# Combine weights and running decay sums turned by VectorE's block transposition and stored in 128-byte pieces

## Chip, cores and metric

The kernel runs on one core of a Trainium2 chip. The time is the device time of one execution in microseconds (us), as the median of several runs. The core's engines work side by side, each on its own list of instructions, and wait for each other through semaphores: TensorE (PE in the profile; PEld is its weight load), VectorE (DVE), ScalarE (ACT), GpSimd (POOL) and SyncE (SP), which here issues DMAs.

## What is computed

32 sequences of 512 tokens and 256 channels go through two residual layers. The first is a state-space mixer; two of its steps matter here: the running sums of the decays, and the factors `exp(sum[l] - sum[s])` built from them. The second layer is a mixture of 16 experts with a shared expert; here the combine weights matter, one per token and expert, which scale the hidden rows of each expert.

```python
Adt = (dt * A)...; Acs = jnp.cumsum(Adt, axis=-1)
Lmat = jnp.exp(segsum(Adt))                      # exp(Acs[l] - Acs[s]) for s <= l
Y_diag = jnp.einsum('bcln,bcsn,bhcls,bcshp->bclhp', Cr, Br, Lmat, xdt)
...
topk_idx, w, _scores = _route(xf, router_w, correction_bias)
combine = jnp.zeros((S, E), xf.dtype).at[jnp.arange(S)[:, None], topk_idx].add(w)
h = _silu(g) * u
hw = h * combine.T[:, :, None]
routed = jnp.einsum('esh,ehc->sc', hw, down_w)
```

## The kernel before

Each engine has a list of steps written out by hand, in stages: `lead`, `first`, 30 steady iterations (one ahead of a loop, 29 in it), `tail`, `drain`, `last`. A steady iteration overlaps three things: the projection of the query for sequence i+1 (part p), the mixer of sequence i (part a), and the experts of sequence i-1 (part f). So every step below runs 32 times, 30 of them in steady iterations. Sequences are split into 4 chunks of 128 tokens; there are 8 heads and 16 experts.

The order of the work on each engine is the order in its `iteration()`. PSUM banks are handed out in turn: `PLANS` lists the fillings of each part, and the filling at place n takes bank n modulo the number of banks (three for a, two for f), after the one that had the bank before was read out (`slot`).

Two small tensors have to be turned, because they arrive with tokens on the partitions and are needed as rows that a DMA can spread over all partitions:

- The decay sums. TensorE's `cumulate` (L1518 to L1520) makes three products into one bank: the sums by token, the totals by a matrix of ones, and the sums again as rows (32 rows of 128 tokens, L1520). VectorE's `evac_acs` copies the rows to `acsT` (L1138), and SyncE's `decay_store` writes them with one DMA to `acs_row` in device memory (L486). `decay_rows` loads them back into `seg`, broadcast over the partitions (L492); GpSimd's `mask` (L607) and ScalarE's `exp_seg` (L845) follow, then VectorE's product with `CBs` (L1167) and TensorE's `diagonal` (L1577). VectorE's `chunk_y` copies out its result (L1193 for the first chunk), and GpSimd's `gated` (L622) goes on from there.
- The combine weights. VectorE's `route_experts` ends with the weights in `gt`, 128 tokens by 4 chunks by 16 experts (L1303). TensorE's `combine_by_expert` turns them with four transposes (L1611) into an f bank `cT`; ScalarE's `evac_cT` copies them to `cT`, a part of `cb` (L895); SyncE's `combine_store` writes them to `c_row` (L497), and `combine_rows` loads, for each block of two experts, the rows back into `cb` (L505). GpSimd's `combine(j)` (L647) multiplies the hidden rows of block j by them.

Around these steps stand, for each of the 12 hidden blocks j: TensorE's `gate(j)` and `up(j)` (L1443 into an f bank), ScalarE's SiLU and VectorE's `up(j)` (L1249), ScalarE's rounding `round_hidden(j)` (L914), GpSimd's `rest(j)` (L652), and TensorE's `down(j)` (L1632). GpSimd's list in the iteration runs `rest(3); combine(4); gated(0); combine(5); ...` to `rest(10); rest(11)`, all in order. At the start of the next iteration TensorE makes `ffn_by_channel` (the transposes of L1462 into f banks).

Of the kernel before, what the change touches and what calls it, by code (L numbers as in the profile page):

```python
# [12 lines left out]
P = 128  # L13
# [5 lines left out]
SB = SH // P  # L19
LAST = 2  # L20
# [12 lines left out]
def build(nc, x, wq_t, wzx_t, conv_w, conv_b, dt_bias, a_log, d_param, npw, ngw, wo_t,  # L33
# [6 lines left out]
    with ctx:  # L40
# [52 lines left out]
        acsT = sb("acsT", [NT * HS, P])  # L93
# [14 lines left out]
        cT = cb[0:E, 0, :]  # L108
# [38 lines left out]
        class Plan:  # L147
# [7 lines left out]
            def filled_count(self, part, engine, upto=None):  # L155
# [56 lines left out]
                    ("cT", "ACT", "ACT"), ("U4", "DVE", "DVE"), ("G5", "ACT", "ACT"), ("U5", "DVE", "DVE"),  # L212
# [7 lines left out]
                    "G0", "G1", "G2", "G3", "G4", "cT", "G5", "G6", "G7", "G8", "G9", "G10", "G11"),  # L220
# [24 lines left out]
                    ("U2", "DVE", "DVE"), ("G3", "ACT", "ACT"), ("U3", "DVE", "DVE"), ("cT", "ACT", "ACT"),  # L245
                    ("G4", "ACT", "ACT"), ("U4", "DVE", "DVE"), ("G5", "ACT", "ACT"), ("U5", "DVE", "DVE"),
# [7 lines left out]
                    "G0", "G1", "G2", "G3", "cT", "G4", "G5", "G6", "G7", "G8", "G9", "G10", "G11"),  # L254
# [9 lines left out]
                    ("G3", "ACT", "ACT"), ("U2", "DVE", "DVE"), ("cT", "ACT", "ACT"), ("G4", "ACT", "ACT"),  # L264
# [5 lines left out]
                    "G0", "G1", "G2", "G3", "cT", "G4", "G5", "G6", "G7", "G8", "G9", "G10", "G11"),  # L270
# [10 lines left out]
        class Way:  # L281
# [34 lines left out]
            "seg_free": ("SP", "a", NT, True), "acs_stored": ("SP", "a", 16, False),  # L316
# [25 lines left out]
            "cT_ready": ("SP", "f", 1, False), "c_stored": ("SP", "f", 16, False),  # L342
# [17 lines left out]
            "c_ready": ("PE", "f", 1, False), "acc_free": ("PE", "f", 1, True),  # L360
# [95 lines left out]
        def _(sp):  # L456
# [27 lines left out]
            def decay_store():  # L484
                sp.wait_ge(sem["acsT_ready"], 1)
                sp.dma_start(acs_row, acsT[:]).then_inc(sem["acs_stored"], 16)  # L486

            def decay_rows(c):
                sp.wait_ge(sem["acs_stored"], 16)

                sp.wait_ge(sem["seg_free"], now("seg_free", c - 1) if c >= 2 else NT - 1 + c)
                sp.dma_start(seg[:, c % 2, :, :].rearrange("p b c -> p (b c)"),  # L492
                             rows(acs_row, [[0, P], [1, HS * P]], c * HS * P)).then_inc(sem[f"seg_loaded{c}"], 16)

            def combine_store():
                sp.wait_ge(sem["cT_ready"], 1)
                sp.dma_start(c_row, cT).then_inc(sem["c_stored"], 16)  # L497

            def combine_rows(r):
                if r == 0:  # L500
                    sp.wait_ge(sem["c_stored"], 16)
# [251 lines left out]
        def _(act):  # L753
# [139 lines left out]
            def evac_cT():  # L893
                way.filled(act, "ACT", "cT")
                own.do(A.copy(cT, way.bank("cT")[0:E, :]))  # L895
                act.sem_inc(sem["cT_ready"], 1)
                freed["f"].append("cT")
                act.sem_inc(sem["f_out_ACT"], 1)

# [65 lines left out]
            def iteration(g=True):  # L965
# [7 lines left out]
                gate(4); evac_CB(); silu_z(2, 1); exp_table(); decays(); evac_cT(); exp_seg(0); round_hidden(3)  # L973
# [11 lines left out]
            def tail():  # L985
# [6 lines left out]
                conv_first(3); silu_z(2, 1); evac_cT(); round_hidden(3); gate(4); conv_silu(3); silu_z(3, 1)  # L992
# [9 lines left out]
            def drain():  # L1002
                begin("drain")
                f_high(0); f_high(1); score_tanh(); gate(0); gate(1); final_norm(); round_hidden(0)
                round_hidden(1); gate(2); gate(3); round_hidden(2); evac_cT(); gate(4); round_hidden(3)
# [25 lines left out]
        def _(dve):  # L1031
# [252 lines left out]
            def route_experts():  # L1284

                for t in range(NT):
# [16 lines left out]
                V.tensor_tensor(gt[:].rearrange(te, t=NT), gt[:].rearrange(te, t=NT),  # L1303
                                ws[:].unsqueeze(2).broadcast_to([P, NT, E]), ALU.mult).then_inc(sem["c_ready"], 1)
# [102 lines left out]
        def _(pe):  # L1407
# [105 lines left out]
            def cumulate():  # L1513
# [5 lines left out]
                nc.tensor.matmul(b[:, n:2 * n], ones[:], rhs, start=True, stop=True)  # L1519
                fill("acs", nc.tensor.matmul(b[0:n, P:2 * P], rhs, upper[:], start=True, stop=True))  # L1520
# [157 lines left out]
            def iteration(g=True):  # L1678
# [8 lines left out]
                gate(4); CB(); x_by_token(0); up(3); down(1); x_by_token(1); combine_by_expert(); down(2)  # L1687
                settled("c_ready"); up(4); gate(5); state(0); project_z(3, 1); diagonal(0); up(5)
# [11 lines left out]
            def tail():  # L1700
# [6 lines left out]
                project_z(2, 1); down(1); combine_by_expert(); gate(4); settled("c_ready"); project_z(3, 1)  # L1707
# [10 lines left out]
            def drain():  # L1718
# [3 lines left out]
                down(0); settled("acc_free"); up(2); down(1); combine_by_expert(); gate(4); settled("c_ready")  # L1722
# [71 lines left out]
```

## Time and profile before

| | us |
|---|---|
| median of 3 runs | 3145.26 (3142.36 to 3146.18) |
| the profiled execution | 3135.33 |
| its span, first to last instruction | 3133.6 |

| engine | busy us | share of the span |
|---|---|---|
| TensorE matmuls | 3057.2 | 98% |
| TensorE weight loads | 2626.1 | 84% |
| VectorE | 2358.9 | 75% |
| ScalarE | 1932.9 | 62% |
| GpSimd | 2034.6 | 65% |

The views are read as follows. The stage table gives each engine's busy time in a stretch of the span. The chain of work that ended last goes back from the last instruction to what released it, step by step, and so tells what set the end. A timeline lists one engine's instructions in order of time; in brackets stand the idle time ahead of one and what ended it. A matmul's length in a timeline includes its way through the array, in which the next one already runs, so pieces of the chain, which run from start to start, are the better price. "issue" in DMA rows is SyncE's own time for handing a DMA over; landing is when its last byte has arrived.

### The profile page before, as it was taken

What the parts mean: (1) busy time and instruction counts of PE and PEld (TensorE: products, weight loads), DVE (VectorE), ACT (ScalarE), POOL (GpSimd) and SP (SyncE); (2) the same over time, 40 slices, a digit from 0 to 9 for tenths busy, and PEclk for the clock granted to TensorE, in tenths of its full rate; (3) what the DMA queues carried; (4) which work ended last, traced back from release to release, by engine and by line L of the source; (5) the groups of instructions that cost most, each with busy time, mean ns of one, the idle gap of its engine ahead of it and who ended that gap; (6) DMA issues with size and microseconds to landing.
All of it is one profiled execution on the core that took longest, in us unless ns stands there. A gap on an engine that the chain in (4) does not pass through costs nothing.

```text
span 3133.6 us, 66479 instructions
## 1 busy us (share of the span) xinstructions
PE 3057.2 (98%) x21696; PEld 2626.1 (84%) x21696; DVE 2358.9 (75%) x5104; ACT 1932.9 (62%) x4149; POOL 2034.6 (65%) x2311
## 2 busy tenths in 40 slices
PE   5799999999999999999999999999999999999997
PEld 4688888888888888888888888888888888888876
DVE  5877777777777777777777777777777778777762
ACT  5466666666666566666666666666666666656562
POOL 2477666677666677666676666676666776666764
PEclk7899999999999999999999999999999999999998
DMA  3122222222222222222222222122222222222221
GB/s 125 42 69 89 74 72 67 68 69 86 76 64 65 74 74 81 78 68 61 70 82 78 80 67 59 67 87 78 78 64 64 67 88 74 81 61 67 68 82 41
DMA packets 143436, 227.37 MB, mean 73 GB/s; under 512 B 18977, under 2 KB 88353, under 8 KB 143393
## 3 DMA queue, kind: packets, MB, share of 16 engines
q1 hardware_dynamic: 126496, 210.06, 20.3%
q0 software_dynamic: 16896, 16.78, 4.0%
q8 instruction: 22, 0.36, 0.0%
q14 instruction: 22, 0.17, 0.0%
HBM read 174.87 MB, written 35.13 MB: 67 GB/s over the span
## 4 chain that ended last, share of the span: by engine, by line
PE 87%; POOL 6%; DVE 1%; issue 1%; DMA 0%; ACT 0%; POOLq 0%; SPq 0%; DVEq 0%; ACTq 0%
PE fpb L1443 32%; PE apb L1443 19%; PE acc L1632 16%; PE apb L1577 4%; PE apb L1452 4%; PE apb L1560 2%; PE ppb L1443 2%; PE apb L1567 2%; PE ppb L1462 1%; POOL hid L647 1%; POOL hidL L652 1%; PE fpb L1492 1%; PE fpb L1494 1%; PE apb L1547 1%; PE fpb L1462 1%
## 5 line engine op out<-in xcount | busy, mean ns | idle before, releaser
L652 POOL TENSOR_TENSOR hidL<-hid,hidH 128x512 fp32r<-128x512 f32 x384 | 545.1, 1420 | 239.5 <-ACT hidH L914 231.6
L1130 DVE SCALAR_TENSOR_TENSOR xc<-apb,cw,xc 128x511 f32<-128x511 f32 (+2 forms) x576 | 427.9, 747 | 66.7 <-ACT xc L827 38.5
L1632 PE MATMUL acc<-WDH,hidH 128*128 128x256 f32 x1536 | 458.2, 298 | 4.6 <-POOLq L654 4.4
L914 ACT CAST hidH<-hid 128x512 fp32r<-128x512 f32 x384 | 236.3, 615 | 365.5 <-POOL hid L647 307.4
L1632 PE MATMUL acc<-WDH,hidL 128*128 128x256 f32 x1536 | 432.3, 281 | 0.0
L1632 PE MATMUL acc<-WDL,hidH 128*128 128x256 f32 x1536 | 431.7, 281 | 0.0
L647 POOL TENSOR_TENSOR hid<-hid,cb 128x512 f32<-128x512 f32 x256 | 348.2, 1360 | 39.7 <-DMA cb<-c_row 15.7
L1249 DVE TENSOR_TENSOR hid<-hid,fpb 128x512 f32<-128x512 f32 x384 | 261.5, 681 | 142.4 <-PE fpb L1443 139.0
L1443 PE MATMUL fpb<-fTh,UH 128*128 128x512 f32 x768 | 336.5, 438 | 0.0
L1443 PE MATMUL fpb<-fTh,GH 128*128 128x512 f32 x768 | 319.6, 416 | 0.0
L845 ACT ACTIVATE seg<-seg,acs 128x128 f32<-128x128 f32 x1024 | 313.7, 389 | 8.9 <-ACT cb L895 5.7
L1632 PEld LDWEIGHTS acc<-WDH,hidH 128*128 128x128 f32 x1536 | 290.4, 189 | 23.3 <-issue 7.4
L1443 PE MATMUL fpb<-fTh,GL 128*128 128x512 f32 x768 | 304.8, 397 | 0.0
L1443 PE MATMUL fpb<-fTh,UL 128*128 128x512 f32 x768 | 303.9, 396 | 0.0
L1443 PE MATMUL fpb<-fTl,GH 128*128 128x512 f32 x768 | 303.8, 396 | 0.0
L1443 PE MATMUL fpb<-fTl,UH 128*128 128x512 f32 x768 | 302.5, 394 | 0.0
L1632 PEld LDWEIGHTS acc<-WDL,hidH 128*128 128x128 f32 x1536 | 291.1, 189 | 12.8 <-issue 7.2
L903 ACT ACTIVATE hid<-fpb 128x512 f32<-128x512 f32 x384 | 228.9, 596 | 116.0 <-PE fpb L1443 75.0
L1632 PEld LDWEIGHTS acc<-WDH,hidL 128*128 128x128 f32 x1536 | 290.4, 189 | 0.0
L622 POOL TENSOR_TENSOR xD<-xD,xdt 128x512 f32<-128x512 f32 x128 | 210.0, 1641 | 23.1 <-DVEq L1196 22.7
L827 ACT ACTIVATE xc<-apb,cbv,cw 128x512 f32<-128x512 f32 x192 | 149.2, 777 | 113.6 <-PE apb L1443 69.8
L1167 DVE TENSOR_TENSOR seg<-seg,CBs 128x1024 f32<-128x1024 f32 x128 | 164.1, 1282 | 43.9 <-ACT seg L845 34.6
(195 smaller groups left out, 8600.9 us busy)
## 6 DMA issues: line engine op xcount, KB each, us to landing
seg<-acs_row SPq DMA_DIRECT2D x128, 512.0 KB, 4.2
cb<-c_row SPq DMA_DIRECT2D x512, 128.0 KB, 2.9
xsP<-in_x SPq DMA_DIRECT2D x32, 512.0 KB, 3.6
xc<-qrot SPq DMA_DIRECT2D x32, 512.0 KB, 3.4
xc<-in_x SPq DMA_DIRECT2D x32, 512.0 KB, 4.5
out<-xc SPq DMA_DIRECT2D x32, 512.0 KB, 3.0
out<-xn POOLq DMA_DIRECT2D x32, 512.0 KB, 6.0
ZL_loaded<-in_wzx_t SPq DMA_DIRECT2D x2, 512.0 KB, 4.5
```

Source lines behind the costliest of these rows:

```text
L622: own.do(G.tensor_tensor(xD[:, c % 2, :], xD[:, c % 2, :], xdt[:, c % 2, :], ALU.add))
L647: G.tensor_tensor(hid[:, j % 2, :], hid[:, j % 2, :], cb[:, r % 2, :], ALU.mult).then_inc(sem["routed_ready"], 1)
L652: own.do(G.tensor_tensor(hidL[:, j % 2, :], hid[:, j % 2, :], hidH[:, j % 2, :].bitcast(fp32), ALU.subtract))
L827: A.activation(xc[:, b, :], way.bank(f"xc{b}")[:], ACT.Identity, bias=cbv[:, b:b + 1], scale=cw[:, b, TAPS - 1:TAPS]).then_inc(sem["conv_f ...
L845: ins = A.activation(seg[:, c % 2, h, :], seg[:, c % 2, h, :], ACT.Exp, bias=acs[:, 0, c * HS + h:c * HS + h + 1])
L903: own.do(A.activation(hid[:, j % 2, :], way.bank(f"G{j}")[:], ACT.Silu))
L914: A.copy(hidH[:, j % 2, :], hid[:, j % 2, :]).then_inc(sem["hidden_high"], 1)
L1130: ins = V.scalar_tensor_tensor(xc[:, b, s:], src[:, 0:T - s], cw[:, b, TAPS - 1 - s:TAPS - s], xc[:, b, s:], ALU.mult, ALU.add)
L1167: V.tensor_tensor(seg[:, c % 2, :, :], seg[:, c % 2, :, :], CBs[:, c, :].unsqueeze(1).broadcast_to([P, HS, P]), ALU.mult).then_inc(sem["m_ ...
L1249: own.do(V.tensor_tensor(hid[:, j % 2, :], hid[:, j % 2, :], way.bank(f"U{j}")[:], ALU.mult))
L1443: ins = nc.tensor.matmul(dst, l, r, start=n == 0, stop=n == total - 1)
L1632: ins = nc.tensor.matmul(dst, l[:, w, tk], r[:, j, :], start=j == 0 and t % 2 == 0 and n == 0, stop=j == HB - 1 and n == 2, skip_group_che ...
```

## The change

TensorE turns neither tensor any more. VectorE's `transpose` turns each 32x32 block of a tile in place: after it, partition 32i+k of the output, column 32j+n, holds partition 32i+n, column 32j+k of the input. So 32 rows of the result hold the values of 32 tokens, in pieces of 32 numbers (128 bytes) that still have to be put together; the store to device memory does this with four DMAs, one for each group of 32 partitions.

- `cumulate` makes two products instead of three. `evac_acs` turns the sums by token (128x32, out of PSUM) into `acsT`, now 128x32, and `decay_store` issues four DMAs.
- `combine_by_expert` (TensorE) and `evac_cT` (ScalarE) are gone, and `cT` with them from the plans and from the f banks' turn: every f filling behind it moves to the other of the two banks. `route_experts` writes the weights to `eq`, ordered by expert, waits for that, and turns them (128x64) into `msk`; `combine_store` waits for VectorE's `c_ready` and issues four DMAs.
- The loads wait for all four stores (`16 * NT`).

```diff
-        acsT = sb("acsT", [NT * HS, P])
+        acsT = sb("acsT", [P, NT * HS])
...
-                    ("cT", "ACT", "ACT"), ("U4", "DVE", "DVE"), ("G5", "ACT", "ACT"), ("U5", "DVE", "DVE"),
+                    ("U4", "DVE", "DVE"), ("G5", "ACT", "ACT"), ("U5", "DVE", "DVE"),
...
             def decay_store():
                 sp.wait_ge(sem["acsT_ready"], 1)
-                sp.dma_start(acs_row, acsT[:]).then_inc(sem["acs_stored"], 16)
+                for i in range(NT):
+                    sp.dma_start(rows(acs_row, [[P, NT * HS], [1, BL]], i * BL), acsT[i * BL:(i + 1) * BL, :]
+                                 ).then_inc(sem["acs_stored"], 16)
...
             def combine_store():
-                sp.wait_ge(sem["cT_ready"], 1)
-                sp.dma_start(c_row, cT).then_inc(sem["c_stored"], 16)
+                sp.wait_ge(sem["c_ready"], 1)
+                for i in range(NT):
+                    sp.dma_start(rows(c_row, [[P, BL], [BL * P, 2], [1, BL]], i * BL),
+                                 msk[i * BL:(i + 1) * BL, :].rearrange("p (j b) -> p j b", j=2)
+                                 ).then_inc(sem["c_stored"], 16)
...
-            def evac_cT():
-                way.filled(act, "ACT", "cT")
-                own.do(A.copy(cT, way.bank("cT")[0:E, :]))
...
-                gate(4); evac_CB(); silu_z(2, 1); exp_table(); decays(); evac_cT(); exp_seg(0); round_hidden(3)
+                gate(4); evac_CB(); silu_z(2, 1); exp_table(); decays(); exp_seg(0); round_hidden(3)
...
-                V.tensor_copy(acsT[:], way.bank("acs")[0:NT * HS, P:2 * P]).then_inc(sem["acsT_ready"], 1)
+                V.transpose(acsT[:], way.bank("acs")[:, 0:NT * HS]).then_inc(sem["acsT_ready"], 1)
...
-                V.tensor_tensor(gt[:].rearrange(te, t=NT), gt[:].rearrange(te, t=NT),
-                                ws[:].unsqueeze(2).broadcast_to([P, NT, E]), ALU.mult).then_inc(sem["c_ready"], 1)
+                own.do(V.tensor_tensor(eq[:].rearrange("p (e t) -> p t e", t=NT), gt[:].rearrange(te, t=NT),
+                                       ws[:].unsqueeze(2).broadcast_to([P, NT, E]), ALU.mult))
+                V.transpose(msk[:], eq[:]).then_inc(sem["c_ready"], 1)
...
-                nc.tensor.matmul(b[:, n:2 * n], ones[:], rhs, start=True, stop=True)
-                fill("acs", nc.tensor.matmul(b[0:n, P:2 * P], rhs, upper[:], start=True, stop=True))
+                fill("acs", nc.tensor.matmul(b[:, n:2 * n], ones[:], rhs, start=True, stop=True))
...
-            def combine_by_expert():
-                b = slot("cT")
-                pe.wait_ge(sem["c_ready"], 1)
-                for t in range(NT):
-                    ins = nc.tensor.transpose(b[0:E, t * P:(t + 1) * P], gt[:, t * E:(t + 1) * E], ident[:])
-                fill("cT", ins)
...
-                gate(4); CB(); x_by_token(0); up(3); down(1); x_by_token(1); combine_by_expert(); down(2)
-                settled("c_ready"); up(4); gate(5); state(0); project_z(3, 1); diagonal(0); up(5)
+                gate(4); CB(); x_by_token(0); up(3); down(1); x_by_token(1); down(2)
+                up(4); gate(5); state(0); project_z(3, 1); diagonal(0); up(5)
```

## Rows read from the trace of the kernel before

**Rows 1.** Stage table, first sequence, then a steady iteration: stretch, busy us (instructions) of engines, TensorE clock, DMA.
```profile
50.00:100.00 50.00, 36.23 (x224) 24.99 (x225) 41.84 (x66) 30.32 (x72) 23.45 (x22) 0.73 0.21 74
...
1552.50:1647.00 94.50, 94.45 (x679) 81.41 (x679) 73.06 (x160) 59.69 (x130) 63.45 (x72) 1.00 0.24 73
```

**Rows 2.** The chain that ended last, in order of time: start, length in us, engine, tile, line.
```profile
1561.26 0.22 PE apb L1519 x2
1561.48 0.34 PE apb L1520 x2
1561.82 1.60 PE fpb L1443 x6
...
1573.60 1.40 PE fpb L1443 x6
...
1576.84 0.44 PE fpb L1611 x4
1577.28 1.43 PE acc L1632 x12
...
1583.07 1.08 PE apb L1577 x32
1584.15 1.59 PE fpb L1443 x6
```

**Rows 3.** The same chain one iteration later, where it runs through GpSimd.
```profile
1678.75 0.70 DVE xdt L1193
1679.67 1.29 POOL xD L622
...
1730.69 1.25 POOL hidL L652
1732.03 1.68 PE acc L1632 x12
```

**Rows 4.** VectorE's timeline: start, length in us, line, operation, idle before it and releaser.
```profile
1562.39 0.17 DVE L1139 TENSOR_SCALAR acs<-apb 128x32 f32<-128x32 f32 x1
...
1575.89 0.23 DVE L1303 TENSOR_TENSOR gt<-gt,ws 128x64 f32<-128x64 f32 x1
1576.04 0.68 DVE L1249 TENSOR_TENSOR hid<-hid,fpb 128x512 f32<-128x512 f32 x1
...
1633.64 0.69 DVE L1249 TENSOR_TENSOR hid<-hid,fpb 128x512 f32<-128x512 f32 x1 [0.17 <-PE fpb L1443]
```

**Rows 5.** ScalarE's timeline around the copy of the turned weights.
```profile
1577.32 0.58 ACT L895 COPY cb<-fpb 16x512 f32<-16x512 f32 x1 [1.46 <-PE fpb L1611]
1578.09 2.46 ACT L845 ACTIVATE seg<-seg,acs 128x128 f32<-128x128 f32 x8 [0.19 <-ACT cb L895]
```

**Rows 6.** SyncE's DMA issues in the same iteration.
```profile
1563.92 0.81 SPq L492 DMA_DIRECT2D seg<-acs_row  x2
1577.96 0.32 SPq L497 DMA_DIRECT2D c_row<-cb  x1
1579.54 1.10 SPq L505 DMA_DIRECT2D cb<-c_row  x2
```

**Rows 7.** GpSimd's timeline in the same iteration.
```profile
1572.09 1.10 POOL L607 TENSOR_SCALAR_AFFINE_SELECT seg<-seg 128x1024 f32<-128x1024 f32 x1 [0.33 <-POOL hidL L652]
...
1583.27 1.27 POOL L647 TENSOR_TENSOR hid<-hid,cb 128x512 f32<-128x512 f32 x1 [0.33 <-DMA cb<-c_row]
1585.23 1.28 POOL L622 TENSOR_TENSOR xD<-xD,xdt 128x512 f32<-128x512 f32 x1 [0.69 <-DVEq L1196]
```

**Rows 8.** DMA issues of the whole run: count, KB each, median us from issue to landing.
```profile
seg<-acs_row SPq DMA_DIRECT2D x128, 512.0 KB, 4.2
cb<-c_row SPq DMA_DIRECT2D x512, 128.0 KB, 2.9
...
c_row<-cb SPq DMA_DIRECT2D x32, 32.0 KB, 1.6
...
acs_row<-acsT SPq DMA_DIRECT2D x32, 16.0 KB, 1.4
```

**Rows 9.** TensorE's timeline: the first FFN transposes behind the turn of the loop.
```profile
1635.12 0.60 PE L1462 MATMUL fpb<-ident,xdt 128*128 128x128 f32 x4
```

More of the change, by code:

```diff
@@ L19 @@
 SB = SH // P
+BL = 32
 LAST = 2
@@ L107, in build @@
         cb = sb("cb", [P, 2, T])
-        cT = cb[0:E, 0, :]
         fst6, fmv = sb("fst6", [P, NT, 6]), sb("fmv", [P, NT, 2])
@@ L219, in build @@
                 ("f", "ACT"): (
-                    "G0", "G1", "G2", "G3", "G4", "cT", "G5", "G6", "G7", "G8", "G9", "G10", "G11"),
+                    "G0", "G1", "G2", "G3", "G4", "G5", "G6", "G7", "G8", "G9", "G10", "G11"),
                 ("p", "ACT"): (
@@ L253, in build @@
                 ("f", "ACT"): (
-                    "G0", "G1", "G2", "G3", "cT", "G4", "G5", "G6", "G7", "G8", "G9", "G10", "G11"),
+                    "G0", "G1", "G2", "G3", "G4", "G5", "G6", "G7", "G8", "G9", "G10", "G11"),
                 ("f", "DVE"): (
@@ L269, in build @@
                 ("f", "ACT"): (
-                    "G0", "G1", "G2", "G3", "cT", "G4", "G5", "G6", "G7", "G8", "G9", "G10", "G11"),
+                    "G0", "G1", "G2", "G3", "G4", "G5", "G6", "G7", "G8", "G9", "G10", "G11"),
                 ("f", "DVE"): (
@@ L315, in build @@
             "x_loaded": ("DVE", "a", 16, False), "acsT_ready": ("SP", "a", 1, False),
-            "seg_free": ("SP", "a", NT, True), "acs_stored": ("SP", "a", 16, False),
+            "seg_free": ("SP", "a", NT, True), "acs_stored": ("SP", "a", 16 * NT, False),
             "conv_first": ("DVE", "a", CB_, False), "ln_ready": ("DVE", "a", 1, False),
@@ L340, in build @@
             "ffn_in_ready": ("PE", "f", 2, False),
-            "cT_ready": ("SP", "f", 1, False), "c_stored": ("SP", "f", 16, False),
+            "c_ready": ("SP", "f", 1, False), "c_stored": ("SP", "f", 16 * NT, False),
             "cb_free": ("SP", "f", NR, True),
@@ L359, in build @@
             "hidden_split": ("PE", "f", HB - LAST, False), "last_split": ("PE", "g", LAST, False),
-            "c_ready": ("PE", "f", 1, False), "acc_free": ("PE", "f", 1, True),
+            "acc_free": ("PE", "f", 1, True),
         }
@@ L991, in tail @@
                 decays(); round_hidden(1); evac_B(); silu_table(); silu_z(1, 1); gate(3); round_hidden(2)
-                conv_first(3); silu_z(2, 1); evac_cT(); round_hidden(3); gate(4); conv_silu(3); silu_z(3, 1)
+                conv_first(3); silu_z(2, 1); round_hidden(3); gate(4); conv_silu(3); silu_z(3, 1)
                 exp_table(); exp_seg(0); exp_seg(1); round_hidden(4); silu_table(); gate(5); gate(6); evac_y(0)
@@ L1004, in drain @@
                 f_high(0); f_high(1); score_tanh(); gate(0); gate(1); final_norm(); round_hidden(0)
-                round_hidden(1); gate(2); gate(3); round_hidden(2); evac_cT(); gate(4); round_hidden(3)
+                round_hidden(1); gate(2); gate(3); round_hidden(2); gate(4); round_hidden(3)
                 gate(5); round_hidden(4); gate(6); round_hidden(5); gate(7); round_hidden(6); gate(8)
@@ L1706, in tail @@
                 settled("ad_ready"); settled("acc_free"); B_by_token(); project_z(1, 1); up(3); project_x(3)
-                project_z(2, 1); down(1); combine_by_expert(); gate(4); settled("c_ready"); project_z(3, 1)
+                project_z(2, 1); down(1); gate(4); project_z(3, 1)
                 up(4); x_by_token(0); gate(5); x_by_token(1); down(2); up(5); state(0); diagonal(0); state(1)
@@ L1721, in drain @@
                 settled("last_split"); logits(0); logits(1); gate(0); gate(1); up(0); up(1); gate(2); gate(3)
-                down(0); settled("acc_free"); up(2); down(1); combine_by_expert(); gate(4); settled("c_ready")
+                down(0); settled("acc_free"); up(2); down(1); gate(4)
                 up(3); down(2); up(4); gate(5); down(3); up(5); gate(6); down(4); up(6); gate(7); down(5)
```

12 lines of the change are left out of this document (4 added, 8 removed).

## Prediction

> **What bounds the kernel now.** I read the stage table first. In a steady iteration TensorE is busy for 94.45 of 94.50 us at granted clock 1.00, the higher of the two levels, while VectorE has 73, ScalarE 60 and GpSimd 63 us of work [rows 1]. The reader is to see that nothing on TensorE's stream is idle: 30 of the 32 sequences run like this, so a microsecond taken out of this stream, with nobody else becoming late, is a microsecond off the iteration. The first sequence is different: TensorE is busy for 36 of 50 us at clock 0.73 [rows 1], so work removed there is worth little.
>
> The chain of work that ended last comes second. It gives the length of each piece of TensorE's stream without the overlap of pipelined matmuls, and it shows what stands beside it [rows 2]. In a later iteration the chain leaves TensorE behind the first diagonal product, goes through VectorE's copy of it to GpSimd at 1679.67 us, and stays on GpSimd until `rest(10)`, which ends at 1731.94 us; `down(10)` starts at 1732.03 us [rows 3]. So GpSimd's 52 us from `gated(0)` to `rest(10)` are as long as TensorE's matmuls beside them. The two pieces that the change removes lie ahead of that fork (cumulate at 1561 us, the expert transposes at 1576 us, the first diagonal product at 1583 us [rows 2]), so both branches start earlier, provided that GpSimd can start `gated(0)` earlier. That is the question of this case, and the engines' timelines around the fork answer it.
>
> **The change part by part.** *TensorE, expert weights.* Four transposes of 128x16 leave: 0.44 us in the chain [rows 2]. Their neighbours before and behind stay and move together, so I take the 0.44 whole; 32 of them give 14.1 us.
>
> *TensorE, decay sums.* The third product of cumulate leaves: 0.34 us [rows 2]. What follows it, six matmuls of `gate(2)`, takes 1.60 us where such a group takes 1.40 elsewhere. That extra 0.20 also stands behind the diagonal product, a row of short products as the `ones` product is, which is to come last (1.59 us [rows 2]), so I expect it to stay. The ends are 0.14 (0.20 more becomes exposed) and 0.54 (the extra goes too); I take 0.34, by that nearest row. 31 of the 32 lie in the stage where TensorE is full: 10.5 us.
>
> Sum on TensorE: 14.1 + 10.5 = 24.6 us, or 0.78 us per steady iteration; with the ends 18 to 31 us.
>
> *ScalarE* loses `evac_cT`, 0.58 us, and 1.46 us of waiting for TensorE ahead of it [rows 5]. `exp_seg(0)`, queued behind, needs only the mask, which GpSimd finished at 1573.2 us [rows 7], so it can start some 2 us earlier. ScalarE is not the bound, so this adds no gain by itself; it makes `m_ready`, the wait of the first diagonal product, earlier, which that product needs if it is to be 0.78 us earlier.
>
> *VectorE.* The decay copy (32x128) becomes a block transposition of 128x32 from PSUM. The trace has no transposition; the next operation reads the same 128x32 from PSUM in 0.17 us [rows 4]. I take 0.2, between 0.17 and that of a 128x512 operation, 0.68. The weights get one more instruction on 128x64, whose neighbour took 0.23 us [rows 4], and a wait for its input: some 0.3 us together, between 0.2 and 0.7. `up(3)` and the two `times_dt` queue behind it. Behind those, the decay product waits for ScalarE, which now comes 2 us sooner, so 0.3 us are hidden. Were that cover gone, 0.3 us would pass to the first diagonal product and cost at most 30 x 0.3 = 9 us.
>
> *The decay stores.* One DMA of 512-byte rows becomes four of 128-byte pieces. On SP the loads of `seg` queue behind them; the next store comes 14 us later [rows 6]. Those loads were issued at 1563.92 us and landed 4.2 us later [rows 6, 8], by about 1568.6 us, and the mask that uses them started at 1572.09 us [rows 7]: 3.5 us of slack. Three more issues at up to 0.55 us, the pitch of the weight row loads [rows 6], and a landing 1.5 us longer (2.9 in place of 1.4, as those loads take [rows 8]) cost 3.2 us. I cost this at nothing.
>
> *The combine stores* are the narrow place. Before: the weights were ready at 1576.12 us [rows 4]; transposes, ScalarE's copy and SP brought the store to 1577.96 us, and the row loads to 1579.54 us [rows 6]: 3.42 us. After: 0.3 us for the transposition, three issues more, one landing. An issue alone is 0.32 us; the pitch in a pair is 0.4 to 0.55 [rows 6]; I take 0.4, since these are small stores like the 0.32. The landing of 128-byte pieces is not in the trace: 512-byte pieces took 1.4 us, 2 KB pieces 1.6, and the row loads 2.9 [rows 8]. I take 1.6, the same tensor's. So 0.3 + 1.2 + 1.6 = 3.1 us, 0.3 us sooner than before. The ends are 2.7 (0.32 pitch, 1.4 landing) and 4.85 us (0.55, 2.9).
>
> What the fork allows: `combine(4)` ran right on the landed rows at 1583.27 us, and `gated(0)` behind it then still waited 0.69 us for VectorE's copy of the diagonal product [rows 7]. The weights become ready 0.34 us earlier (cumulate lies ahead of them), and `gated(0)` wants to be 0.78 us earlier, so the gain is whole as long as the path of the weights grows by no more than 0.69 + 0.34 - 0.78 = 0.25 us; it is gone at 1.03 us. My 3.1 us is well inside, the upper end of +1.43 us is outside.
>
> The Trainium skill speaks against the stores. "DMA: Bandwidth & Descriptors", Specifications, says that pieces under 512 B make the DMA engine read, modify and write; its section on the anatomy of one DMA puts the fixed cost at about 2 us, mostly the receipt of the write. The rows stand below that figure. With 2.0 us landing, an estimate by that page, the path would be 3.5 us, +0.1, and the sum would stand; what the read-modify-write adds for so few pieces no row here shows.
>
> *PSUM slots.* Without `cT` the later slots of the two f banks swap parity. `gate(5)` now waits for VectorE's `up(3)`, which ends at 1576.72 us, while `gate(5)` comes two groups behind 1577.28 us [rows 2, 4]. At the turn of the loop the first FFN transposes wait for `up(11)` instead of `G11`: `up(11)` ended at 1634.33 us, the transposes started at 1635.12 us [rows 4, 9]. With the 0.22 us that GpSimd needed from the end of VectorE's copy to its own start [rows 3] this leaves 0.5 us, and `up(11)` itself follows TensorE. I cost it at nothing; missed by 0.3 us in each iteration it would cost 9 us.
>
> **The rivals.** (a) *The path of the weights holds the fork.* If stores land in about 2.5 us at a 0.4 us pitch, the path is 4.0 us, +0.58: 0.33 us of each 0.78 are lost, 30 x 0.33 = 10 us, and the time is 3131. For: GpSimd's branch is as long as TensorE's. Against: measured stores took 1.4 and 1.6 us.
>
> (b) *The same path makes the kernel slower.* From +1.03 us on, the iteration is longer than before. At the upper end, +1.43, it is 0.40 us longer: 30 x 0.40 = 12 us, 3157 us. It needs both upper ends at once. For: sub-512-byte writes are not in the trace. Against: only 64 pieces of 128 bytes per store.
>
> (c) *The turn of the loop or VectorE's longer routing eats part*, 9 us as worked out above: 3130.
>
> (d) *No gain*, as GpSimd's branch decides alone and is not started earlier: 3145. Against: `gated(0)` waited on TensorE's product, not on GpSimd [rows 7].
>
> **How the numbers follow.** The profiled execution took 3135.33 us (span 3133.6), so it would come to 3110.7. The median of the runs is 9.9 us higher; a difference of stages carries over, and 3145.26 - 24.6 = 3120.7, so I forecast 3121. Its own range is 3114 to 3127 by the ends of the sum on TensorE. Chances: forecast 0.72, (a) 0.08, (c) 0.06, (d) 0.06, (b) 0.08. The range of 8 in 10 reaches from 3114 over (a) and (c) to 3137. This kernel's measurement can tell about 0.2%, 6 us, from no change: faster 0.86, same 0.06, slower 0.08.
>
> **What the profile of the changed kernel should show.** TensorE's span per iteration at 93.7 us, still full; no L1520 or L1611 products, with `x_by_token(1)` running straight into `down(2)`; `exp_seg(0)` some 2 us earlier against TensorE; the row loads no later against the end of the routing than 3.4 us; `gated(0)` still waiting for VectorE and not `combine(4)` for a DMA; transpositions of 0.2 us; no new idle of TensorE at the first FFN transposes. I am wrong if the last of the four combine stores lands over 2.2 us after its issue, or if the transposition takes over 0.7 us.

## The result, and the profile after

The changed kernel takes 3105.15 us (median of 4 runs, 3103.29 to 3106.31) against 3143.81 us for the kernel before beside it (4 runs, 3141.42 to 3146.18): ratio 0.988, 95% interval 0.987 to 0.989. The forecast was 3121 us with a range down to 3114, so the sign was right and the size too small by 16 us. On three later chips the changed kernel gave 3106.24, 3105.02 and 3106.77 us, the kernel before 3137.20, 3128.17 and 3143.69 us: it is the kernel before that varies. That turns out to be part of the answer.

The profiled execution took 3105.57 us (span 3103.9), 29.8 us less than that of before. The stage table of after, the first sequence and one steady iteration (columns as in [rows 1]):

```profile
50.00:100.00 50.00, 34.91 (x240) 25.52 (x241) 42.60 (x67) 31.08 (x73) 24.89 (x22) 0.76 0.21 75
1546.60:1640.30 93.70, 93.57 (x674) 80.67 (x674) 73.69 (x161) 59.14 (x129) 64.10 (x72) 1.00 0.24 73
```

TensorE looks as full as in [rows 1], 93.57 of 93.70 us. That is misleading, as the chain of waits shows: first the shares of the chain that ended last, by engine, of before, then of after.

```profile
PE 87%; POOL 6%; DVE 1%; issue 1%; DMA 0%; ACT 0%; POOLq 0%; SPq 0%; DVEq 0%; ACTq 0%
```

```profile
PE 44%; POOL 43%; issue 4%; DMA 3%; DVE 1%; SPq 1%; POOLq 0%; ACT 0%; DVEq 0%; ACTq 0%
```

The kernel before is set by TensorE almost alone: GpSimd's 6% are its branch in the four iterations that took 0.4 us longer, in one of which [rows 3] lie, and a piece of the last stages. The changed kernel is set by TensorE and GpSimd in turn. One iteration of that chain in after (start, length, engine, tile, line), against [rows 2, 3]:

```profile
1546.33 0.14 PE apb L1516 x2
1546.47 0.22 PE apb L1517 x2
1546.70 1.48 PE fpb L1441 x6
...
1561.15 0.44 PE apb L1450 x4
1561.59 1.41 PE acc L1622 x12
...
1567.37 1.11 PE apb L1574 x32
1568.61 0.70 DVE xdt L1190
1569.53 1.28 POOL xD L626
...
1620.33 1.25 POOL hidL L656
1621.68 1.66 PE acc L1622 x12
```

From the `ones` product to the end of `gate(2)` before took 0.22 + 0.34 + 1.60 = 2.16 us [rows 2]; it now takes 0.22 + 1.48 = 1.70, so the third product was worth 0.46. The four expert transposes (0.44 [rows 2]) are gone, and `x_by_token(1)` (L1450) runs straight into `down(2)`. From VectorE's copy of the first diagonal product to `down(10)` the branch over GpSimd takes 1621.68 - 1568.61 = 53.07 us, before 1732.03 - 1678.75 = 53.28 [rows 3]. In this iteration `down(10)` waits for it. How long TensorE's weight loads waited there for GpSimd in the steady iterations (us in total, times, longest), of before, then of after:

```profile
PEld acc L1632 <- POOLq L654: 1.2, 4, 0.4
```

```profile
PEld acc L1622 <- POOLq L658: 8.7, 28, 0.3
```

The new operations and the stores are where they were expected. VectorE's timeline (against [rows 4]), SyncE's issues ([rows 6]), ScalarE's first `exp_seg` ([rows 5]), GpSimd's timeline ([rows 7]) and the landings ([rows 8]) of after:

```profile
1547.42 0.22 DVE L1135 STREAM_TRANSPOSE acsT<-apb 128x32 f32<-128x32 f32 x1
...
1560.65 0.28 DVE L1300 TENSOR_TENSOR eq<-gt,ws 128x64 f32<-128x64 f32 x1
1560.96 0.24 DVE L1302 STREAM_TRANSPOSE msk<-eq 128x64 f32<-128x64 f32 x1
```

```profile
1547.67 1.73 SPq L486 DMA_DIRECT2D acs_row<-acsT  x4
1550.45 0.82 SPq L493 DMA_DIRECT2D seg<-acs_row  x2
1561.24 1.74 SPq L499 DMA_DIRECT2D c_row<-msk  x4
1564.04 1.10 SPq L509 DMA_DIRECT2D cb<-c_row  x2
```

```profile
1560.52 2.44 ACT L849 ACTIVATE seg<-seg,acs 128x128 f32<-128x128 f32 x8
```

```profile
1567.66 1.27 POOL L651 TENSOR_TENSOR hid<-hid,cb 128x512 f32<-128x512 f32 x1 [0.33 <-DMA cb<-c_row]
1569.53 1.27 POOL L626 TENSOR_TENSOR xD<-xD,xdt 128x512 f32<-128x512 f32 x1 [0.60 <-DVEq L1193]
1570.89 1.28 POOL L627 TENSOR_TENSOR zs<-zs,xD 128x512 f32<-128x512 f32 x1
1572.49 1.89 POOL L651 TENSOR_TENSOR hid<-hid,cb 128x512 f32<-128x512 f32 x1 [0.33 <-POOL zs L627]
1574.34 1.73 POOL L656 TENSOR_TENSOR hidL<-hid,hidH 128x512 fp32r<-128x512 f32 x1
...
1581.67 1.08 POOL L588 TENSOR_TENSOR pnb<-pnb,prstd 128x4 f32<-128x4 f32 x1
```

```profile
cb<-c_row SPq DMA_DIRECT2D x512, 128.0 KB, 2.9
...
acs_row<-acsT SPq DMA_DIRECT2D x128, 4.0 KB, 1.5
...
c_row<-msk SPq DMA_DIRECT2D x128, 8.0 KB, 1.5
```

The routing's weights are ready at 1560.93 us and the row loads are issued at 1564.04: 3.1 us, before 3.42 us [rows 4, 6].

Where the 29.8 us went: I take the iteration's length from one `evac_acs` to the next. The 29 steady intervals lost 24.2 us (2740.5 to 2716.3 us), the first interval 1.9 (90.05 to 88.12), the one into the tail 1.1 (99.67 to 98.54), and what follows the last `evac_acs` 2.3 (148.7 to 146.4).

### The profile page after: what moved, and what is told of

Its sections match the earlier page's. It is cut to its first block, busy times and chain, and to the rows that moved or that the text cites. A ratio compares the mean times of both kernels' runs of the same rounds, so it can differ in the third digit from the quotient of the medians.

```text
span 3103.9 us, 66159 instructions
## 1 busy us (share of the span) xinstructions
PE 3022.7 (97%) x21504; PEld 2598.2 (84%) x21504; DVE 2379.3 (77%) x5136; ACT 1914.6 (62%) x4117; POOL 2049.9 (66%) x2311
## 4 chain that ended last, share of the span: by engine, by line
PE 44%; POOL 43%; issue 4%; DMA 3%; DVE 1%; SPq 1%; POOLq 0%; ACT 0%; DVEq 0%; ACTq 0%
PE fpb L1441 17%; PE apb L1441 12%; POOL hidL L656 9%; POOL hid L651 9%; PE acc L1622 8%; POOL xD L626 5%; POOL zs L627 4%; POOL rstd L587 3%; DMA cb<-c_row 2%; POOL qrot L600 2%; POOL seg L611 2%; PE apb L1450 1%; POOL ry L592 1%; POOL rq L592 1%; POOL ve L586 1%
## 5 line engine op out<-in xcount | busy, mean ns | idle before, releaser
L656 POOL TENSOR_TENSOR hidL<-hid,hidH 128x512 fp32r<-128x512 f32 x384 | 559.5, 1457 | 199.6 <-ACT hidH L911 191.7
L1164 DVE TENSOR_TENSOR seg<-seg,CBs 128x1024 f32<-128x1024 f32 x128 | 178.9, 1398 | 12.6 <-ACT seg L849 3.2
```

The costliest lines, as they stand in the source:

```text
L656: own.do(G.tensor_tensor(hidL[:, j % 2, :], hid[:, j % 2, :], hidH[:, j % 2, :].bitcast(fp32), ALU.subtract))
L1164: V.tensor_tensor(seg[:, c % 2, :, :], seg[:, c % 2, :, :], CBs[:, c, :].unsqueeze(1).broadcast_to([P, HS, P]), ALU.mult).then_inc(sem["m_ ...
```

## The experiments

All lengths of an iteration are measured from `evac_acs` to `evac_acs` in steady iterations. The eighteen runs came in seven groups, each on one chip and beside the kernel before there.

**The kernel before, again.** No edit.

> The kernel before, unchanged, to profile another execution of it. Its profiled execution took 3135 us, the median of its runs 3144. Theory A (GpSimd's branch from gated(0) to rest(10) decides many iterations in a usual execution): where an execution takes about 3144 us, most steady iterations are 94.85 us long instead of 94.44, with down(10) waiting 0.4 us for rest(10); in the first profile only 5 of 29 were. Theory B (a general difference of pace between executions): all iterations are longer by about 0.3 us, with no wait at down(10). The time stays at 3141 to 3146.

3129.04 us, ratio 1.0004 (0.9994 to 1.0013) to the kernel before on this chip. All steady iterations but one took 94.45 us, that one 94.92. So 94.45 is the usual length here, and 3144 us is not the kernel's only time. The expected 3141 to 3146 us did not come, so the run decides between neither theory.

**One GpSimd operation moved to VectorE,** on the kernel before and on the changed one.

```diff
-    ... mask(2); decayed(2)          # GpSimd
+    ... mask(2)
+    if c == NT - 2:                  # VectorE, times_dt(2)
+        V.tensor_tensor(by_head(xdec...), by_head(xdt...), along(ed[:, c, :]), ALU.mult)
```

> The kernel before with the product of chunk 2 for the state (decayed(2), 1.04 us) taken from GpSimd's branch and given to VectorE behind times_dt(2). Theory A: GpSimd's branch is 1 us shorter, the 0.4 us waits at down(10) go, and the median falls by about 9 us to 3133 to 3137, steady iterations all at 94.44 us. Theory B: TensorE is full anyway, the median stays at 3141 to 3147.

> The changed kernel with the same move of decayed(2) to VectorE. Its TensorE waits 0.3 us for rest(10) in each iteration, and its matmul stream ahead of that is 1.16 us shorter than before. Theory A (GpSimd's branch now decides): the waits at down(10) go, steady iterations fall from 93.68 to about 93.25 us, the time to 3090 to 3096. Rival (the wait only moves, because TensorE is held next by ScalarE's or VectorE's steps around the turn of the loop, or VectorE gets late): iterations at 93.6 us or more, 3102 to 3110.

Both missed: 3158.9 us, ratio 1.010 (1.0085 to 1.0118), 95.4 us an iteration, and 3132.9 us, ratio 1.001 (0.9998 to 1.0018), 94.4 us: each some 0.7 to 1.0 us an iteration longer than without the edit. GpSimd's timeline of the second shows why:

```profile
1594.38 0.19 POOL L585 TENSOR_SCALAR pnb<-pmv 128x4 f32<-128x4 f32 x1 [1.58 <-DVE pmv L1064]
```

VectorE's own operations behind the added one became later, GpSimd's norm now waits 1.58 us for one of them (in after 0.28), and the branch is longer though it has an operation less. The edit was too blunt to say whether GpSimd's work bounds the changed kernel. But it showed that lateness at the branch's end goes straight into the time.

**Each half of the change alone.** The expert weights by VectorE with the decay sums left to TensorE, and the reverse.

```diff
-    ("cT", "ACT", "ACT"), ...                    # weights only
+    V.transpose(msk[:], eq[:])
-    fill("acs", nc.tensor.matmul(b[0:n, P:2 * P], rhs, upper[:], ...))      # sums only
+    V.transpose(acsT[:], way.bank("acs")[:, 0:NT * HS])
```

> Only the half of the change for the combine weights; the decay sums as before (third product, one store). TensorE loses 0.46 us per iteration. If each half gives its own TensorE time: steady iterations 0.45 us shorter, 15 us in all, to 3126 to 3131. Theory A: the weights' half also lets the waits at down(10) go, as GpSimd's gated(0) starts earlier against TensorE's later matmuls no more than before, so the same 15 us and hardly more. Rival (the freed ScalarE and the earlier rows carry the whole effect): 3105 to 3112, as with both halves.

> Only the half of the change for the decay sums; the weights as before, through TensorE and ScalarE. TensorE loses 0.46 us per iteration ahead of the fork. Fork theory (GpSimd's branch takes back what lies beyond it): with the weights' half alone iterations went from 94.45 to 94.00 us, with both to 93.68, so this half alone gives 94.0 us, 13 to 16 us in all. Rival (its gain depends on the earlier exp_seg(0) of the other half): 94.2 us or more, under 9 us.

Weights alone: 3116.32 us, ratio 0.9955 (0.9939 to 0.9972), 94.00 us an iteration, 0.45 less than 94.45; the 0.44 of the sum stands. Sums alone: 3120.46 us, ratio 0.9945 (0.9929 to 0.9962), 94.11 us, 0.34 less. This is just the 0.34 forecast, but not for the reason given, for here TensorE already waits for GpSimd in 28 of the 29 intervals. The one without the wait took 93.72 us, so on TensorE alone this half is worth 0.73:

```profile
PEld acc L1634 <- POOLq L657: 8.7, 28, 0.3
```

**The changed kernel again.** No edit.

> The changed kernel, unchanged, beside the kernel before on one chip again. First comparison: 3143.8 to 3105.2 us, 38.7 us less, while the two first profiles differ by 29.8 us. Theory P (the change is worth what its stages show; steady iterations 0.76 us shorter make 22 us of it, first and last stages some 5 us, and the remaining 9 us lay in the executions of the kernel before that were timed first): 24 to 30 us less than the kernel before here, ratio 0.990 to 0.993. Theory Q (the full 38 us are the change's, wherever it is measured): ratio 0.988 or below.

3106.24 us, ratio 0.990 (0.989 to 0.992): 31 us less than the kernel before there, just above the 24 to 30 of theory P. Its profiled execution was the quickest of the four, 3093.75 us, and has both lengths: 93.25 to 93.30 us in 21 steady intervals, 93.64 to 93.67 in 7, one of 93.52. GpSimd's timeline in a short iteration and then in the next, a long one:

```profile
486.60 0.19 POOL L586 TENSOR_SCALAR ve<-mv 128x2 f32<-128x2 f32 x1
486.87 0.75 POOL L587 TENSOR_TENSOR rstd<-ve,mhalf 128x2 f32<-128x2 f32 x1
...
579.88 0.52 POOL L586 TENSOR_SCALAR ve<-mv 128x2 f32<-128x2 f32 x1
580.48 0.82 POOL L587 TENSOR_TENSOR rstd<-ve,mhalf 128x2 f32<-128x2 f32 x1
```

and VectorE's, beside them:

```profile
486.58 0.87 DVE L1216 SCALAR_TENSOR_TENSOR xc<-xc,rstd 128x256 f32<-128x256 f32 x2
...
579.86 0.87 DVE L1216 SCALAR_TENSOR_TENSOR xc<-xc,rstd 128x256 f32<-128x256 f32 x2
```

Two iterations equal to 0.02 us up to here part at one small GpSimd operation of `norm_x1(0)`: it takes 0.52 instead of 0.19 us, the next 0.07 more, and all of GpSimd's work behind is 0.40 us later, `rest(10)` and with it `down(10)` too. Both times VectorE's `add_x(1)` starts 0.02 us ahead of it. In after's own profile the operation takes 0.47 to 0.50 us, and 93.68 us is the rule there. The two lengths of the kernel before part at the same operation. Its profile, in an iteration of 94.44 us and in the next, one of 94.83 us, that of [rows 3]:

```profile
1630.62 0.19 POOL L582 TENSOR_SCALAR ve<-mv 128x2 f32<-128x2 f32 x1
...
1725.05 0.51 POOL L582 TENSOR_SCALAR ve<-mv 128x2 f32<-128x2 f32 x1
```

**Four more stores ahead of the combine stores,** to a second tensor that nobody reads, so that the rows land later.

```diff
-    for i in range(NT):
-        sp.dma_start(rows(c_row, ...), msk[i * BL:(i + 1) * BL, :]...)
+    for i, dst in [(i, r) for r in (c_row2, c_row) for i in range(NT)]:
+        sp.dma_start(rows(dst, ...), msk[i * BL:(i + 1) * BL, :]...)
```

> The changed kernel with four more stores of the weights, to a tensor that nobody reads, ahead of the four: the row loads come 4 x 0.43 = 1.7 us later. Fork theory: gated(0) waited 0.60 us behind combine(4), so 1.1 us of the 1.7 pass into GpSimd's branch and from there into every iteration: 94.8 us, 33 us more than the changed kernel, slower than the kernel before. Rival (the path of the weights is not on the branch, other waits hide it): within 6 us of the changed kernel.

3120.25 us, 14 us over the changed kernel, 94.0 us an iteration: 0.33 longer, between the rival's nothing and the 1.1 that the sum at the fork gives. GpSimd's timeline in one such iteration:

```profile
1857.12 1.28 POOL L652 TENSOR_TENSOR hid<-hid,cb 128x512 f32<-128x512 f32 x1 [2.13 <-DMA cb<-c_row]
...
1859.70 2.25 POOL L628 TENSOR_TENSOR zs<-zs,xD 128x512 f32<-128x512 f32 x1
1862.28 1.36 POOL L652 TENSOR_TENSOR hid<-hid,cb 128x512 f32<-128x512 f32 x1 [0.33 <-POOL zs L628]
1863.60 1.26 POOL L657 TENSOR_TENSOR hidL<-hid,hidH 128x512 fp32r<-128x512 f32 x1
...
1870.46 0.41 POOL L589 TENSOR_TENSOR pnb<-pnb,prstd 128x4 f32<-128x4 f32 x1
```

`combine(4)` waits 2.13 us for the rows, as meant (in after 0.33), and 0.60 of the 1.80 more falls into the wait that `gated(0)` had. The second step of `gated(0)` (L628) then takes 0.97 us more than in after. But `combine(5)`, `rest(4)` and the last step of `norm_px`, which took 1.89, 1.73 and 1.08 us in after, take 1.36, 1.26 and 0.41: 1.67 us come back. All of these now fall beside other VectorE operations. A delay on GpSimd's branch is not passed on one for one.

**`decayed(2)` at a later place on VectorE,** behind `moments_px`, in the steady iterations.

> The changed kernel with decayed(2) of the steady iterations given to VectorE, this time behind moments_px, so that GpSimd's norm_px does not wait for VectorE. Fork theory: GpSimd's branch is 1.05 us shorter, the 0.3 us wait at down(10) goes, iterations at 93.25 to 93.4 us, 8 to 12 us less than the changed kernel. Rival (VectorE's later up(6), chunk_y(2) and decay products bring the wait back elsewhere): 93.7 us or more.

3110.75 us, 93.74 us an iteration, no gain over the changed kernel, as the rival had it. The wait for GpSimd is gone, and another stands in its place: `diagonal(2)` on TensorE waits 0.36 us in each iteration for VectorE's decay product of that chunk (L1169). VectorE's product, in one iteration, and TensorE's waits in the steady iterations:

```profile
1486.80 2.16 DVE L1169 TENSOR_TENSOR seg<-seg,CBs 128x1024 f32<-128x1024 f32 x1
```

```profile
PE apb L1579 <- DVE seg L1169: 10.5, 29, 0.4
```

The product took 1.23 us in after (L1164, last section). Behind the added operation it starts later and takes longer.

**GpSimd's branch shortened without touching VectorE.** `rope_sum(1)` adds 32 of 256 columns, which makes its operation some 1.1 us shorter; VectorE's list stays as it is.

```diff
+                w = 32 if s else D
-                G.tensor_tensor(qrot[:, pair(s), :], qrot[:, pair(s), :], xn[:, pair(s), :], ALU.add
+                G.tensor_tensor(qrot[:, pair(s), 0:w], qrot[:, pair(s), 0:w], xn[:, pair(s), 0:w], ALU.add
```

> The kernel before, unchanged, to get a profiled execution of it on another chip. Theory (the iteration has two lengths, 0.40 us apart, by whether GpSimd's first small operation of the gate norm meets a VectorE operation): each steady iteration is 94.45 or 94.85 us and nothing between; a time near 3128 us goes with 94.45 nearly throughout, a time near 3140 us with 94.85 nearly throughout. Rival (the kernel before has one length, 94.45, and its median differs between chips for another reason, such as a slower head or clock): 94.45 in nearly all iterations even where the time is near 3140 us.

> The kernel before with GpSimd's rope_sum(1) adding only 32 of 256 columns of each of its blocks (part of the rotation of q is left out of the second half), which makes GpSimd's branch about 1.1 us shorter per iteration and leaves VectorE alone. Theory: at 94.45 us an iteration of before is bounded by TensorE, at 94.85 by GpSimd's branch with its collision, so all steady iterations fall to 94.45 us: no gain where before ran at 94.45, 0.4 x 30 = 12 us where before ran at 94.85. Rival (GpSimd bounds nothing in before): the same time as the kernel before, whatever its length.

> The changed kernel with the same shortened rope_sum(1). Theory: the changed kernel waits at down(10) for GpSimd's rest(10), so with GpSimd's branch 1.1 us shorter that wait goes and the period falls from 93.68 us to what TensorE's own stream allows, 93.27 us, some 12 us less in all than the changed kernel: against the kernel before 94.45 - 93.27 = 1.18 us an iteration where that is at 94.45. Rival (the bound at 93.68 is TensorE's own, the wait on GpSimd a coincidence): 93.68 us, the changed kernel's time.

> The changed kernel, unchanged, on the same chip as the three runs beside it, so that the shortened rope_sum(1) is judged against the changed kernel and not only against the kernel before. Theory: 93.68 us in nearly all iterations, some 3106 us; an iteration of 93.27 us where the collision on GpSimd misses. Rival (the two lengths belong to chips and not to executions): one length throughout, whichever it is.

The kernel before: 3128.42 us, 94.45 us in every steady iteration. With the edit: 3126.8 us, ratio to the kernel before 0.9995 (0.9985 to 1.0004), 94.43 us. The changed kernel: 3105.02 us, 93.67 us from the fourth steady interval on (ahead of that 93.20 to 93.31). With the edit: 3092.69 us, 93.22 us throughout, and its chain that ended last is TensorE's again:

```profile
PE 93%; POOL 1%; DVE 1%; DMA 1%; ACT 0%; issue 0%; SPq 0%; DVEq 0%; POOLq 0%; ACTq 0%
```

So TensorE alone is worth 94.43 - 93.22 = 1.21 us an iteration in this change, and GpSimd's branch takes 0.45 of it back. The rival (a coincidence) is out.

**The kernel before where it takes longer.** Ten of the missing microseconds were the kernel before's own: 3145 us as the median that the forecast started from, 3135 in the profiled execution. The same edit was run beside it three more times.

> The kernel before, unchanged, once more for a profiled execution. Theory (two lengths of the iteration, by the meeting of GpSimd's first small operation with VectorE): 94.45 or 94.85 us and nothing between, and the time of the execution follows the count of the long ones, 0.40 us each. Rival (slower executions of the kernel before are slower ahead of the loop, or by the clock): 94.45 in nearly all iterations also in an execution near 3140 us.

> The kernel before with GpSimd's rope_sum(1) adding only 32 of 256 columns of each of its blocks, once more, beside the kernel before on this chip. Theory: some 3127 us on every chip, as it removes what GpSimd's meeting with VectorE costs; so the same time as the kernel before where that is near 3128 us, and 10 to 12 us less where that is near 3140 us. Rival (slower executions of the kernel before have nothing to do with GpSimd): the same time as the kernel before here, wherever that is.

> The kernel before with the shortened rope_sum(1), once more, for a chip on which the kernel before takes longer than the 3128 to 3129 us of the last ones. Theory: some 3125 us on every chip, so that the gain over the kernel before is the larger the slower that is: 4 us at 3129, 12 us at 3137, and no more than 12 us (30 iterations of 0.40 us) however slow. Rival (slower executions of the kernel before have nothing to do with GpSimd): the same gain of some 4 us wherever the kernel before is.

> The kernel before with the shortened rope_sum(1), again for a chip on which the kernel before takes longer than 3130 us. Theory: some 3125 us on every chip, so that the gain over the kernel before grows with the time of that, up to 12 us (30 iterations of 0.40 us). Rival (slower executions of the kernel before have nothing to do with GpSimd): a gain of some 4 us wherever the kernel before is, as on the last two chips.

The profiled execution of before on the first of these (3130.64 us) had 7 intervals of 94.83 to 94.85 us among 22 of 94.42 to 94.47, and as many waits:

```profile
PEld acc L1632 <- POOLq L654: 2.0, 7, 0.3
```

The table has all four pairs (us; ratio to the kernel before with its interval):

| the kernel before | with the shorter `rope_sum(1)` | ratio |
|---|---|---|
| 3128.17 | 3126.80 | 0.9995 (0.9985 to 1.0004) |
| 3129.28 | 3123.92 | 0.9985 (0.9976 to 0.9995) |
| 3127.94 | 3124.30 | 0.9988 (0.9978 to 0.9998) |
| 3140.11 | 3124.81 | 0.9950 (0.9930 to 0.9969) |

With the shorter GpSimd branch the kernel before takes 3124 to 3127 us everywhere; where it was at 3140, 15 us go. Thirty long iterations account for 30 x 0.40 = 12 us. That the excess of the kernel before hangs on GpSimd's branch is shown. The granted clock bears on the rest. Where the kernel before was at 3140, its four executions with a mean granted clock of 0.993 took 3127.42 to 3140.11 us, and the three with 0.988 to 0.991 took 3143.15 to 3145.70. With the edit, in the first row, executions at 0.988 took 3129.53 to 3131.24 us and those at 0.994 took 3123.22 to 3123.83. So the remaining 3 us are probably the clock's; it is not shown, since no profiled execution of the kernel before was above 3136 us.

**A version without the wait that leaves nothing out.** `rope_sum(1)` moves to VectorE, right behind `rope(1)`, where VectorE then idled 0.96 us.

```diff
-    root_y(1); rope_sum(1); rest(9); ...          # GpSimd
+    root_y(1); rest(9); ...
+    if s:                                         # VectorE, rope(s)
+        own.do(ins)
+        V.tensor_tensor(qrot[:, pair(s), :], qrot[:, pair(s), :], xn[:, pair(s), :], ALU.add)
```

> The changed kernel with rope_sum(1) moved whole from GpSimd (1.29 us there) to VectorE, right behind rope(1), in every stage; nothing is left out. Before mixed_out(1) VectorE idles 0.96 us, so 0.7 to 0.9 us more of work there should be covered, and all that is behind it on GpSimd comes up to 1.2 us earlier. Theory (GpSimd's branch alone holds the changed kernel at 93.68 us): 93.2 to 93.3 us an iteration, 12 us less than the changed kernel, some 3093 us. Rival (as when decayed(2) was moved: VectorE becomes late for TensorE or for GpSimd's norms): 93.7 us or more, 3105 to 3115 us.

> The changed kernel, unchanged, on the same chip, so that the moved rope_sum(1) is judged against it: 93.67 us in most iterations and some 3105 us. If it is quicker, the share of 93.27 us iterations is to be that much higher: 0.40 us each.

3092.65 us (3089.48 to 3095.05), ratio to the kernel before 0.984 (0.982 to 0.985); the changed kernel beside it 3106.77 us, 0.989 (0.987 to 0.990). An iteration takes 93.23 us, and only 2 waits for GpSimd are left:

```profile
PEld acc L1627 <- POOLq L658: 0.4, 2, 0.2
```

VectorE's timeline shows the cover: the added operation (L1090) ends at 1508.5 us, and `mixed_out(1)` (L1207), which in after waited 0.96 us for TensorE, starts without a wait.

```profile
1507.82 0.69 DVE L1090 TENSOR_TENSOR qrot<-qrot,xn 128x512 f32<-128x512 f32 x1
1508.43 0.61 DVE L1098 TENSOR_SCALAR xn<-qrot,rq 128x256 f32<-128x256 f32 x2
1509.19 0.88 DVE L1207 SCALAR_TENSOR_TENSOR xc<-apb,ry,xc 128x256 f32<-128x256 f32 x2
```

This is the quickest version here, 14 us ahead of the changed kernel.

## Why the prediction was right in sign and wrong in size

*The step that failed* is the last but one: "a difference of stages carries over" from the profiled execution to the median. The 9.9 us between the two in the kernel before are not a constant beside the stages. The changed kernel has a median 0.4 us below its profiled execution, so 10.3 of the 16 us are lost in this step alone. The two profiles show iterations of different kinds: 25 of 29 are short in before (94.45 us), all but two are long in after (93.68). Compared like with like, the change is worth 94.45 - 93.27 (the one short iteration in the profile of after) = 1.18 us an iteration, or 94.85 - 93.68 = 1.17 where both are long. The sum had 0.78, so over 30 iterations some 12 us were missing in it, and the term at fault is TensorE's, that of the decay sums (below). That the executions behind the first median were mostly of the long kind is inferred from their time; what is shown is that on a later chip 15 us go from 3140 with the shorter GpSimd branch. The profile had the sign of it: among 29 intervals of 94.4 us stood 4 of 94.83 to 94.92, and TensorE waited for GpSimd 4 times. The prediction left the second length out, and took [rows 3], which lie in a long iteration, for the usual course. Where the kernel before ran short, at 3128.17 us, the gain was 23.2 us, near the 24.6 forecast; that is luck, as it sets a short kernel before against a long changed one.

*The other 5 us*: the steady intervals lost 24.2 us, where 29 x 0.78 = 22.6, so 1.6 of the 5.2 lie there. The rest lies outside: the first interval, the one into the tail and the end lost 1.9, 1.1 and 2.3 us, where the sum leaves 2. Only the tail's 1.1 is the same in all eight profiles of the two unchanged kernels (99.67 to 99.71 us before, 98.50 to 98.54 after). All that lies outside the steady intervals took 386 to 393 us in the four profiles of the kernel before, 384 to 390 in those of the changed kernel, and the 393 is that of the first profile, which had the lowest granted clock (0.986 on the mean; 0.991 in after). So the first interval and the end cannot be put down to the change.

*TensorE, expert weights:* 0.44 forecast, 0.45 by the run with this half alone. Right.

*TensorE, decay sums:* 0.34 forecast, 0.46 measured in the chain; the extra 0.20 behind the row of short products went by 0.12, which the upper end of 0.54 had allowed. Over a whole iteration without a wait it is 0.73, beyond that end: this is the term that was too small.

*The sum on TensorE* was 0.78 an iteration; it is 1.21. The missing 0.3 us beyond 0.44 + 0.46 are spread over the groups of matmuls as hundredths of a microsecond, and come with the half for the decay sums (0.73 there, 0.45 with the weights alone). What makes them quicker is open.

*The period* of 93.7 us came out, 93.68, but by luck, as two errors cancel: TensorE gave 0.43 more than the sum, and GpSimd's branch took 0.45 back, 0.40 of it by the meeting at one small operation. I compared `gated(0)` at the fork and asked whether it would start early enough. It did (0.60 us of wait for VectorE left, before 0.69 [rows 7]). I did not ask how much slack the 52 us behind it had against TensorE. It was next to none: lateness of 0.40 us in one small operation already showed in the kernel before.

*The combine stores:* 3.1 us forecast, 3.1 measured; pitch 0.43 us (1.74 for four issues) where I took 0.4, landing 1.5 where I took 1.6. Rivals (a) and (b) needed landings of 2.5 us and more, and fall. The landing stays under the fixed cost of about 2 us that the Trainium skill gives ("DMA: Bandwidth & Descriptors", the anatomy of one DMA). That section is on DMAs that GpSimd issues, which the prediction did not say; these are SyncE's. Pieces of 128 bytes landed 0.1 us from the 512-byte and 2 KB pieces of before [rows 8], so the read-modify-write below 512 bytes that the page's Specifications name shows in no row here. The price of 1 us lost for 1 us of late rows, on which (a) and (b) rested, was too high as well: 0.33 us an iteration was lost for rows behind four more issues of 0.43 us, 1.7 us later.

*VectorE:* transpositions of 0.22 and 0.24 us (0.2 forecast), multiplication and transposition together 0.55 from 1560.65 to 1561.20, where I allowed 0.3 more than the 0.23 of before. Right. Rival (c) is out: no new idle time of TensorE at the first FFN transposes (0.3 us once in the steady iterations, as before), and none for the decay rows. *ScalarE:* `exp_seg(0)` starts 1560.52 - 1546.47 = 14.05 us behind the `ones` product, before 1578.09 - 1561.26 = 16.83 [rows 2, 5]: 2.8 us earlier, where I had said 2. Rival (d), GpSimd alone, was the nearest to what happened: its branch does decide, but from 0.76 us of gain on, not from nothing.

## What to carry to other kernels

Where two engines' branches are equally long between a fork and a join, work removed from one pays only as far as the other has slack. Measure that slack at the join, not at the fork, and shorten the other branch in the same change if its work fits into an idle engine: here that gave 14 us more. If a kernel's steady iterations have more than one length, find what separates them before adding the distance of profile and median to a forecast, and compare iterations of the same kind, since a profile of each kernel may show different ones. And price the removal of a row of short products from the chain up to the end of the group behind it, not by the product's own piece.

## What the runs showed of the hardware

A GpSimd operation on 128x2 values takes 0.19 us alone and 0.46 to 0.52 us when VectorE's two-input operation on 128x256 has started some hundredths of a microsecond ahead of it. In the eight profiles of the two unchanged kernels it was held 106 times in this place, and each time it ended 0.53 us behind the start of the first of VectorE's two operations, which are 0.47 to 0.48 us long, also where it started 0.18 us behind and so took 0.35. It was never held where it started ahead of VectorE's, always from 0.016 us behind on, and either way below that. Such a meeting moves the whole kernel by up to 12 us (30 iterations of 0.40). The Trainium skill, "SBUF — State Buffer", Who interferes with whom, says that a VectorE instruction with two SBUF inputs contends with a GpSimd instruction that reads SBUF, over a pair of ports that is an exclusive lock, and that the order of issue decides who blocks. The trace agrees: GpSimd's operation is held as long as VectorE's first one lasts, or not at all.

The same shows in larger pieces: GpSimd's 128x512 multiplication took 1.27 to 1.89 us, and a 128x4 one 0.41 to 1.08. The latter ended 0.05 us behind VectorE's decay product in after and 0.06 us behind it in the run with four more stores, though it started 0.20 us behind the product's start in the one and 0.88 in the other. VectorE's product of after, then of that run:

```profile
1581.47 1.23 DVE L1164 TENSOR_TENSOR seg<-seg,CBs 128x1024 f32<-128x1024 f32 x1
```

```profile
1869.58 1.23 DVE L1165 TENSOR_TENSOR seg<-seg,CBs 128x1024 f32<-128x1024 f32 x1 [0.70 <-ACT seg L850]
```

A 32x32 block transposition of 128x32 values from PSUM took 0.22 us and one of 128x64 from SBUF 0.24 us, about what an element-wise operation of that size takes (0.17 to 0.23 [rows 4]).
